# Where VectorE takes the first image's attention reciprocals: behind 62 and 68 tap operations, or behind 92 and 98

## The chip, the cores and the metric

The kernel runs on one core of a Trainium2 chip. The metric is the device time of one execution in microseconds (us), as the median of several runs. The engines are TensorE (PE, its weight loads PEld), VectorE (DVE), ScalarE (ACT), GpSimd (POOL) and SyncE (SP, which issues the DMAs).

## What is computed

Eight images x of 256 channels and 32 x 32 pixels pass through a multi-scale linear attention and a feed-forward part with routed experts. Cut to what matters here:

```python
qkv = conv2d(x_normed, qkv_w)                         # 1x1, 768 channels
agg = conv2d(qkv, agg_dw_w, groups=768, padding=2)    # 5x5 taps, channel by channel
agg = conv2d(agg, agg_pw_w, groups=96)                # 1x1 within groups of 8
ms = jnp.concatenate([qkv, agg], axis=1)              # raw half, aggregated half
q, k = relu(t[..., :8]), relu(t[..., 8:16]); v = t[..., 16:]
v = jnp.concatenate([v, ones], axis=-1)
kv = jnp.einsum('bhnd,bhne->bhde', k, v)
out = jnp.einsum('bhnd,bhde->bhne', q, kv)
out = out[..., :-1] / (out[..., -1:] + EPS_ATT)
x = x + batch_norm(conv2d(out, proj_w))
t = t + sum_e weight[b, e] * (gelu(norm(t) @ W1[e] + b1[e]) @ W2[e] + b2[e])
```

The last component of `out` is the denominator of the attention. In the kernel its reciprocals are those that the change moves.

## The kernel before, in words

The program is written engine by engine. Each engine has its own list of instructions, and they meet through semaphores. One list, `ORDER`, made by `schedule()`, gives the order of the pieces of work, and PE, ACT and POOL each walk through it and do their own part of each piece. Every piece that goes through PSUM uses one of two banks (`wbk`) in turn: PE fills it, ACT drains it. So what comes late on PE holds up all that stands behind it in the list.

DVE doesn't follow `ORDER`. It does the 5 x 5 taps. The six channel tiles m of an image are worked on in three pairs, in the order 1, 2, 0 (`PAIRS`): m = 2, 3, then m = 4, 5, then m = 0, 1. For each tap and each m of the pair there is one operation, `tap_ops(s)`, numbered n from 0. In the first image (s = 0) pair 1 is 52 operations (0 to 51), pair 2 is 40 (52 to 91) and pair 0 is 40 (92 to 131). Except for pair 1 of the first image, some taps (`base`) are made by ACT and POOL into `dwo`, and the centre operation of each m (L1104) takes them in. The other taps (L1112) add to `dacc` in PSUM; the last two of each m write `dwo`. A few small tasks stand between the taps at fixed numbers: `OF_LAST` gives those of the image before, `OF_THIS` those of this image. `("rden", h, c)` is `rden_task` (L1013 to L1016): it waits until the attention products `att` of half h (0 raw, 1 aggregated) and of four token blocks c have been drained by ACT, and takes the reciprocal of `den` for them.

```python
def rden_task(s, h, c):
    dve.wait_ge(bank_drained, drained(("att", s, h, (c + 1) * (CH // P) - 1)))
    tl = slice(c * (CH // P), (c + 1) * (CH // P))
    nc.vector.reciprocal(den[:, tl], den[:, tl]).then_inc(rden_made[h], 1)
```

What waits for it: POOL's `scale_att` (L910) multiplies `kt` by the reciprocals, and PE's `back` (L618) transposes the product, which ACT drains (L807). In the first image `ORDER` goes on, for PE and ACT, in this sequence:

1. `att` of the raw half (PE L611, ACT L803 and L804), `scale`, `back` of the raw half
2. `agg` of m = 2, 3 (PE L584), which reads DVE's pair 1
3. `qkv` of m = 2, 3 of the next image (PE L533, ACT L781), the norm of the image after that (POOL L867, L869, PE L635, POOL L875 to L883, PE L644, POOL L889), with base taps of the next image (ACT L700 and L705, POOL L924 and L930) in between
4. `agg` of m = 4, 5, which reads DVE's pair 2, and `qkv` of m = 4, 5 of the next image
5. `kv` of the aggregated half (PE L599, ACT L799), with the next image's base taps, and its mask (POOL L901, L902)
6. `agg` of m = 0, 1 (PE L579, ACT L788), which reads DVE's pair 0, then `att` of the aggregated half, `scale`, `qkv` of m = 0, 1, `back`, `proj` and so on

The feed-forward work of an image (PE L533 and L546, ACT L825, L730 and L731, POOL L960) is filled in between such pieces from the second image on.

On DVE, operations 16 and 21 of the next image have the reciprocals of the aggregated half (`OF_LAST`) ahead of them. POOL's part of `ORDER` holds the scales, the base adds, the norm's sums and products and the mask, in the same sequence. DMAs play no part around the change: the loads of x have their own waits and are issued by SP.

Of the kernel before, what the change touches and what calls it, by code (L numbers as in the profile page):

```python
# [64 lines left out]
def base_taps(s, m):  # L65

    return (0 if m in (2, 3) else len(BASE_TAPS)) if s == 0 else 3
# [8 lines left out]
def tap_ops(s):  # L76

    return [(pair, tap, m) for pair in PAIRS for tap in tap_order(s, pair) for m in (2 * pair, 2 * pair + 1)]
# [200 lines left out]
def taps_before(s, pair):  # L279

    done = sum(len(tap_ops(i)) for i in range(s))
    return done + sum(2 * len(tap_order(s, p)) for p in PAIRS[:PAIRS.index(pair)])
# [33 lines left out]
def build(nc, x, w_qkv, w_dw, w_pw, w_proj, bn, bn_rows, w_router, w1, b1, w2, b2, parts, out):  # L316
    with ExitStack() as ctx:
# [133 lines left out]
        def drained(it):  # L451

            return FILL[it] + 1

        def clip(tap):

            dy, dx = tap // TAPS - TAPS // 2, tap % TAPS - TAPS // 2
            oy, iy, ny = max(0, -dy), max(0, dy), HH - abs(dy)
            ox, ix, nx = max(0, -dx), max(0, dx), WW - abs(dx)
            return (slice(oy, oy + ny), slice(ox, ox + nx)), (slice(iy, iy + ny), slice(ix, ix + nx))  # L460
# [504 lines left out]
        def _(dve):  # L965
# [47 lines left out]
# [5 lines that stand above are left out]
            def max_task(s):  # L1018

                dve.wait_ge(bank_drained, drained(("logits", s)))  # L1020
                dve.sem_inc(dve_gate, 1)
                nc.vector.max(mx[:], lg[:]).then_inc(route, 1)
                dve.wait_ge(route, s * ROUTE + 1)
                dve.sem_inc(dve_gate, 1)
                nc.vector.max_index(ix[:], mx[:], lg[:]).then_inc(route, 1)
                nc.vector.tensor_scalar(rt[:, 0:1], mx[:, 0:1], -1.0, None, ALU.mult).then_inc(max_made, 1)

            def route_task(j):

                dve.wait_ge(exp_made, j * 2 + 2)  # L1030
                nc.vector.reciprocal(rt[:, 4:5], rt[:, 1:2]).then_inc(route, 1)
                dve.wait_ge(route, j * ROUTE + 3)

                nc.vector.tensor_scalar(rt[:, 6:8], rt[:, 2:4], rt[:, 4:5], None, ALU.mult, ALU.add,
                                        accum_out=rt[:, 8:9]).then_inc(route, 1)
                nc.vector.tensor_copy(rt[:, 12:14], ix[:, 0:2]).then_inc(route, 1)
                dve.wait_ge(route, j * ROUTE + 5)
                nc.vector.reciprocal(rt[:, 9:10], rt[:, 8:9]).then_inc(route, 1)
                dve.wait_ge(route, j * ROUTE + 6)
                nc.vector.tensor_scalar(rt[:, 10:12], rt[:, 6:8], rt[:, 9:10], None, ALU.mult).then_inc(route, 1)  # L1040
                dve.wait_ge(route, j * ROUTE + 7)
                for i in range(2):
                    ins = nc.vector.tensor_scalar(wsel[:, i, :], iota11[:], rt[:, 12 + i:13 + i], rt[:, 10 + i:11 + i],
                                                  ALU.is_equal, ALU.mult)
                ins.then_inc(route, 1)
                dve.wait_ge(route, j * ROUTE + 8)
                nc.vector.tensor_tensor(wsel[:, 0, :], wsel[:, 0, :], wsel[:, 1, :], ALU.add).then_inc(route, 1)
                dve.wait_ge(route, j * ROUTE + 9)

            def ew_task(j, par):  # L1050
                nc.vector.tensor_tensor(ewt[:], pws[:], wsel[:, 0, :].unsqueeze(1).to_broadcast([P, FT + E, NP_]),
                                        ALU.mult).then_inc(ew_chain, 1)
                dve.wait_ge(ew_chain, j * 2 + 1)
                nc.vector.reduce_sum(ewr[:], ewt[:], axis=AX_X).then_inc(ew_chain, 1)
                dve.wait_ge(ew_chain, j * 2 + 2)

                nc.vector.scalar_tensor_tensor(out=ews[par][:], in0=ewr[:], scalar=1e-6, in1=ewr[:],
                                               op0=ALU.is_gt, op1=ALU.mult).then_inc(route, 1)
                dve.wait_ge(route, j * ROUTE + 10)
                nc.vector.tensor_tensor(obt[:], b2s[:], ews[par][:, FT:FT + E].unsqueeze(1).to_broadcast([P, CT, E]),  # L1060
                                        ALU.mult).then_inc(route, 1)
                dve.wait_ge(route, j * ROUTE + 11)
                nc.vector.reduce_sum(obs[par][:], obt[:], axis=AX_X).then_inc(route, 1)
                dve.wait_ge(route, j * ROUTE + 12)
                nc.vector.tensor_scalar(ewg[par][:], ews[par][:], G_SCALE, None, ALU.mult).then_inc(route, 1)  # L1065

            def small_task(what, s):
                if what[0] == "rden":
                    rden_task(s, what[1], what[2])
                elif what[0] == "max":  # L1070
                    max_task(s)
                else:
                    route_task(s)
                    ew_task(s, s % 2)


            OF_LAST = {16: ("rden", 1, 0), 21: ("rden", 1, 1), 76: ("max",), 84: ("route",)}
            OF_THIS = {62: ("rden", 0, 0), 68: ("rden", 0, 1)}

            for s in range(B + 1):  # L1080
                if s == B:
                    for n in sorted(OF_LAST):
                        small_task(OF_LAST[n], s - 1)
                    continue
                for n, (pair, tap, m) in enumerate(tap_ops(s)):
                    if n in OF_LAST and s > 0:
                        small_task(OF_LAST[n], s - 1)
                    if n in OF_THIS:
                        small_task(OF_THIS[n], s)
                    no = taps_before(s, PAIRS[0]) + n  # L1090
                    a3 = dacc[:, m % 2, :].rearrange("p (y x) -> p y x", x=WW)
                    o3 = dwo[:, m, :].rearrange("p (y x) -> p y x", x=WW)
                    i3 = qkvs[:, m, :].rearrange("p (y x) -> p y x", x=WW)
                    if no > 1:

                        dve.wait_ge(taps, no - 1)
                    if tap is None:
                        ins = nc.vector.tensor_copy(o3[:, :, WW - 1:WW], a3[:, :, WW - 1:WW])
                    elif tap == CENTER:
                        w = dww[:, m, tap:tap + 1]  # L1100
                        if base_taps(s, m):

                            dve.wait_ge(tap_added, BASE_NO[s, m, base_taps(s, m) - 1])
                            ins = nc.vector.scalar_tensor_tensor(out=dacc[:, m % 2, :], in0=qkvs[:, m, :], scalar=w,  # L1104
                                                                 in1=dwo[:, m, :], op0=ALU.mult, op1=ALU.add)
                        else:
                            dve.wait_ge(bank_drained, drained(("qkv", s, m, NCH - 1)))
                            ins = nc.vector.tensor_scalar(dacc[:, m % 2, :], qkvs[:, m, :], w, None, ALU.mult)
                    else:
                        (oy, ox), (jy, jx) = clip(tap)  # L1110
                        dst = o3 if tap == LAST_TAP else a3
                        ins = nc.vector.scalar_tensor_tensor(  # L1112
                            out=dst[:, oy, ox], in0=i3[:, jy, jx], scalar=dww[:, m, tap:tap + 1],
                            in1=a3[:, oy, ox], op0=ALU.mult, op1=ALU.add)
                    ins.then_inc(taps, 1)
# [60 lines left out]
```

## Time and profile before

| | |
|---|---|
| median of 3 runs | 1648.99 us (1647.67 to 1650.25) |
| the profiled execution, its own time | 1651.42 us |
| its span | 1649.7 us |
| mean granted TensorE clock | 0.934 |
| busy: PE, DVE, ACT, POOL | 1360.8, 1278.6, 1063.1, 972.8 us |
| share of the span | 82%, 78%, 64%, 59% |

The profile is of one execution. The span is what the trace covers; the execution's own time is 1.7 us longer. A busy PE is not PE at its peak, since matmuls overlap. A timeline row gives the start, the length, the engine, the line, the operation with its tiles and how many were merged; in brackets, how long the engine was idle before it and what released it.

### The profile page before, as it was taken

The numbers are of one execution on the slowest core, as the hardware profiler recorded it, in microseconds if no ns is written. First come the engines' busy times: TensorE is split into PE (matmuls) and PEld (weight loads), VectorE is DVE, ScalarE is ACT, GpSimd is POOL, SyncE is SP. The second block draws the span as 40 slices with busy tenths as digits, with TensorE's granted clock in tenths as the row PEclk, the third lists the DMA queues.
The fourth block names the chain that finished last, engine by engine and source line by source line (L and its number), as shares of the span: only waits on it lengthen the run. The fifth ranks groups of instructions, "written<-read, shape, count | busy, mean of one in ns | idle before, by whom it ended". The sixth has DMA issues, their size and how long they took to land.

```text
span 1649.7 us, 18712 instructions
## 1 busy us (share of the span) xinstructions
PE 1360.8 (82%) x6844; PEld 786.7 (48%) x6844; DVE 1278.6 (78%) x1305; ACT 1063.1 (64%) x1855; POOL 972.8 (59%) x746
## 2 busy tenths in 40 slices
PE   4516647799888988799888988899888997999598
PEld 2315525455455545455455545555464445545343
DVE  4895999997969966996969966996969987970000
ACT  3434534677567775767567776777567866675476
POOL 3683626576487566576477566676476647444544
PEclk8756879899999999999999999899999999999899
DMA  5100000000001000010001100010001000100000
GB/s 180 77 2 25 26 0 1 1 27 13 1 1 39 31 9 1 0 64 14 1 1 39 39 1 1 1 39 13 1 1 39 13 1 1 39 13 1 0 14 26
DMA packets 14251, 32.75 MB, mean 20 GB/s; under 512 B 2384, under 2 KB 5328, under 8 KB 13904
## 3 DMA queue, kind: packets, MB, share of 16 engines
q1 hardware_dynamic: 14160, 31.56, 5.5%
q8 instruction: 54, 0.88, 0.2%
q14 instruction: 37, 0.30, 0.1%
HBM read 23.17 MB, written 8.39 MB: 19 GB/s over the span
## 4 chain that ended last, share of the span: by engine, by line
PE 46%; DVE 19%; ACT 19%; POOL 9%; issue 6%; DMA 1%; SPq 0%; POOLq 0%; ACTq 0%; DVEq 0%
PE wbk L533 19%; DVE dacc L1112 15%; PE acc L546 11%; PE wbk L625 6%; ACT gh L730 4%; ACT hb L731 4%; POOL dwo L930 3%; PE wbk L635 3%; ACT tapb L705 2%; POOL nrm L889 1%; PE wbk L584 1%; ACT hb L825 1%; PE wbk L611 1%; ACT dwo L700 1%; PE wbk L599 1%
## 5 line engine op out<-in xcount | busy, mean ns | idle before, releaser
L1112 DVE SCALAR_TENSOR_TENSOR dacc<-qkvs,dww,dacc 128x930 f32<-128x930 f32 (+4 forms) x954 | 1053.2, 1186 | 0.0
L960 POOL TENSOR_TENSOR gl<-hb,gh 128x512 f16<-128x512 f32 x256 | 304.4, 1191 | 419.1 <-ACT hb L731 418.2
L825 ACT ACTIVATE hb<-wbk,b1s 128x512 f32<-128x512 f32 x256 | 175.2, 684 | 156.3 <-PE wbk L533 156.2
L930 POOL TENSOR_TENSOR dwo<-dwo,tapb 128x992 f32<-128x992 f32 (+1 forms) x104 | 240.4, 2311 | 12.9 <-ACT tapb L705 9.7
L546 PE MATMUL acc<-gh,w2h 128*128 128x512 f16 x512 | 197.6, 386 | 33.5 <-ACT sum_b L764 30.6
L546 PE MATMUL acc<-gh,w2l 128*128 128x512 f16 x512 | 197.9, 387 | 0.0
L546 PE MATMUL acc<-gl,w2h 128*128 128x512 f16 x512 | 197.9, 386 | 0.0
L730 ACT ACTIVATE gh<-hb,ewg 128x512 f16<-128x512 f32 x256 | 182.3, 712 | 9.5 <-DVE ewg L1065 9.5
L533 PE MATMUL wbk<-th,w1h 128*128 128x512 f16 x512 | 154.2, 383 | 33.7 <-ACT qr L807 16.7
L731 ACT ACTIVATE hb<-hb,ewg 128x512 f32<-128x512 f32 x256 | 181.8, 710 | 0.0
L1016 DVE RECIPROCAL den<-den 128x128 f32<-128x128 f32 x32 | 30.4, 949 | 189.1 <-ACT den L804 189.1
L533 PE MATMUL wbk<-tl,w1h 128*128 128x512 f16 x512 | 153.5, 382 | 0.0
L533 PE MATMUL wbk<-th,w1l 128*128 128x512 f16 x512 | 153.4, 381 | 0.0
L705 ACT ACTIVATE tapb<-qkvs,dww 128x1024 f32<-128x1024 f32 x104 | 118.2, 1143 | 23.0 <-POOL dwo L930 20.0
L781 ACT ACTIVATE qkvs<-wbk 128x512 f32<-128x512 f32 x96 | 56.5, 594 | 73.6 <-PE wbk L533 73.6
L546 PEld LDWEIGHTS acc<-gh,w2h 128*128 128x128 f16 x512 | 50.6, 99 | 99.6 <-issue 37.6
L910 POOL TENSOR_TENSOR kt<-kt,den 128x1024 f32<-128x1024 f32 x32 | 62.7, 1968 | 59.6 <-DVE den L1016 59.6
L611 PE MATMUL wbk<-kvm,qr 128*128 128x144 f32 x512 | 81.9, 300 | 18.1 <-ACT den L804 12.9
L948 POOL TENSOR_TENSOR yr<-yr,sum_b 128x512 f32<-128x512 f32 x32 | 40.8, 1276 | 88.4 <-ACT sum_b L810 87.5
L1104 DVE SCALAR_TENSOR_TENSOR dacc<-qkvs,dww,dwo 128x1024 f32<-128x1024 f32 x46 | 87.0, 1934 | 0.0
L611 PEld LDWEIGHTS wbk<-kvm,qr 128*128 128x128 f32 x512 | 70.8, 193 | 31.6 <-ACT den L804 21.0
L533 PEld LDWEIGHTS wbk<-th,w1h 128*128 128x128 f16 x512 | 45.9, 98 | 83.8 <-ACT qr L807 20.0
(146 smaller groups left out, 2232.1 us busy)
## 6 DMA issues: line engine op xcount, KB each, us to landing
xa<-x SPq DMA_DIRECT2D x8, 1024.0 KB, 5.0
yr<-x SPq DMA_DIRECT2D x8, 1024.0 KB, 5.0
out<-yr SPq DMA_DIRECT2D x16, 512.0 KB, 2.8
dwo<-w SPq DMA_DIRECT2D x1, 2048.0 KB, 11.0
yr<-w SPq DMA_DIRECT2D x2, 1024.0 KB, 16.3
dwo<-w_qkv SPq DMA_DIRECT2D x1, 768.0 KB, 4.7
wp<-w_proj SPq DMA_DIRECT2D x1, 512.0 KB, 12.4
pw<-w_pw SPq DMA_DIRECT2D x16, 24.0 KB
```

The lines of the kernel that those rows point to most:

```text
L533: last = nc.tensor.matmul(dst, w[:, k, m * P:(m + 1) * P], d[:, k, c * CH:(c + 1) * CH], start=(i == 0), stop=(i == len(parts) - 1))
L546: last = nc.tensor.matmul(acc[:, m, :], w[:, t, m * P:(m + 1) * P], d[:, f % GB, :], start=(t == 0 and i == 0), stop=(t == FT - 1 and i == 2),
L611: last = nc.tensor.matmul(b[:, g * RD:(g + 1) * RD], qr[:, g, t * P:(t + 1) * P], kvm[:, g, :], start=True, stop=True)
L625: last = nc.tensor.matmul(b[:], wp[:, k, m * P:(m + 1) * P], (ac, qr)[k // CT][:, k % CT, c * CH:(c + 1) * CH], start=(k == 0), stop=(k == ...
L705: ins = nc.scalar.activation(tapb[:, i % 2, :], qkvs[:, m, :], ACT.Copy, scale=w)
L730: nc.scalar.activation(gh[:, f % GB, :], hb[:, f % GB, :], ACT.Copy, scale=w).then_inc(g_high, 1)
L731: nc.scalar.activation(hb[:, f % GB, :], hb[:, f % GB, :], ACT.Copy, scale=w).then_inc(g_scaled, 1)
L825: last = nc.scalar.activation(hb[:, f % GB, :], b[:], ACT.Gelu, bias=b1s[:, f % FT:f % FT + 1], scale=1.0 / (X_SCALE * W_SCALE))
L930: ins = nc.gpsimd.tensor_tensor(d3[:, oy, ox], d3[:, oy, ox], t3[:, iy, ix], ALU.add)
L960: nc.gpsimd.tensor_tensor(gl[:, f % GB, :], hb[:, f % GB, :], gh[:, f % GB, :], ALU.subtract).then_inc(g_low, 1)
L1104: ins = nc.vector.scalar_tensor_tensor(out=dacc[:, m % 2, :], in0=qkvs[:, m, :], scalar=w, in1=dwo[:, m, :], op0=ALU.mult, op1=ALU.add)
L1112: ins = nc.vector.scalar_tensor_tensor(out=dst[:, oy, ox], in0=i3[:, jy, jx], scalar=dww[:, m, tap:tap + 1], in1=a3[:, oy, ox], op0=ALU.mu ...
```

## The change

For the first image alone, the two reciprocals of the raw half stand ahead of tap operations 92 and 98 in place of 62 and 68. All other images keep 62 and 68.

```diff
             OF_LAST = {16: ("rden", 1, 0), 21: ("rden", 1, 1), 76: ("max",), 84: ("route",)}
             OF_THIS = {62: ("rden", 0, 0), 68: ("rden", 0, 1)}
+            OF_FIRST = {92: ("rden", 0, 0), 98: ("rden", 0, 1)}
...
-                    if n in OF_THIS:
-                        small_task(OF_THIS[n], s)
+                    if n in (OF_FIRST if s == 0 else OF_THIS):
+                        small_task((OF_FIRST if s == 0 else OF_THIS)[n], s)
```

The added line moves the numbers of all lines behind it by one: the centre operation is L1104 before and L1105 after, the taps are L1112 and L1113.

The first place is DVE's list at the start of pair 2 of the first image: the centre operations, then the taps. `den` holds the denominators. Before:

```order
L1104 SCALAR_TENSOR_TENSOR dacc<-qkvs,dww,dwo 128x1024 x2
L1112 SCALAR_TENSOR_TENSOR dacc<-qkvs,dww,dacc 128x30x30 x2
L1112 SCALAR_TENSOR_TENSOR dacc<-qkvs,dww,dacc 128x30x31 x4
L1112 SCALAR_TENSOR_TENSOR dacc<-qkvs,dww,dacc 128x30x30 x2
L1016 RECIPROCAL den<-den 128x128
L1112 SCALAR_TENSOR_TENSOR dacc<-qkvs,dww,dacc 128x31x30 x2
L1112 SCALAR_TENSOR_TENSOR dacc<-qkvs,dww,dacc 128x31x31 x4
L1016 RECIPROCAL den<-den 128x128
L1112 SCALAR_TENSOR_TENSOR dacc<-qkvs,dww,dacc 128x31x30 x2
```

After:

```order
L1105 SCALAR_TENSOR_TENSOR dacc<-qkvs,dww,dwo 128x1024 x2
L1113 SCALAR_TENSOR_TENSOR dacc<-qkvs,dww,dacc 128x30x30 x2
L1113 SCALAR_TENSOR_TENSOR dacc<-qkvs,dww,dacc 128x30x31 x4
L1113 SCALAR_TENSOR_TENSOR dacc<-qkvs,dww,dacc 128x30x30 x2
L1113 SCALAR_TENSOR_TENSOR dacc<-qkvs,dww,dacc 128x31x30 x2
L1113 SCALAR_TENSOR_TENSOR dacc<-qkvs,dww,dacc 128x31x31 x4
L1113 SCALAR_TENSOR_TENSOR dacc<-qkvs,dww,dacc 128x31x30 x2
```

Both reciprocals have left this stretch, and the taps stand one behind the other.

The second place is DVE's list at the end of pair 2 and the start of pair 0 of the same image. Before:

```order
L1112 SCALAR_TENSOR_TENSOR dwo<-qkvs,dww,dacc 128x32x31 x2
L1098 COPY dwo<-dacc 128x32 x2
L1104 SCALAR_TENSOR_TENSOR dacc<-qkvs,dww,dwo 128x1024 x2
L1112 SCALAR_TENSOR_TENSOR dacc<-qkvs,dww,dacc 128x30x30 x2
L1112 SCALAR_TENSOR_TENSOR dacc<-qkvs,dww,dacc 128x30x31 x4
L1112 SCALAR_TENSOR_TENSOR dacc<-qkvs,dww,dacc 128x30x30 x2
```

After:

```order
L1113 SCALAR_TENSOR_TENSOR dwo<-qkvs,dww,dacc 128x32x31 x2
L1099 COPY dwo<-dacc 128x32 x2
L1016 RECIPROCAL den<-den 128x128
L1105 SCALAR_TENSOR_TENSOR dacc<-qkvs,dww,dwo 128x1024 x2
L1113 SCALAR_TENSOR_TENSOR dacc<-qkvs,dww,dacc 128x30x30 x2
L1113 SCALAR_TENSOR_TENSOR dacc<-qkvs,dww,dacc 128x30x31 x2
L1016 RECIPROCAL den<-den 128x128
L1113 SCALAR_TENSOR_TENSOR dacc<-qkvs,dww,dacc 128x30x31 x2
```

The first reciprocal is now ahead of the centre operations of pair 0, the second behind these and four more taps. The lists of PE, ACT and POOL hold the same instructions in the same order before and after.

## Rows read from the trace of the kernel before

**Rows 1.** Windows, middle: stretch, us, busy us of PE, PEld, DVE, ACT, POOL, PEclk, DMA

```profile
330.00:1500.00 1170.00, 1053.98 (x5417) 605.07 (x5417) 993.87 (x1014) 821.37 (x1464) 727.85 (x560) 0.98 0.04 16
```

**Rows 2.** DVE's waits, whole run: us in total, times, the longest in us

```profile
DVE den L1016 <- ACT den L804: 189.1, 15, 19.9
```

**Rows 3.** Timeline of DVE: start us, us, engine, line, operation, tiles, count, [idle before <-releaser]

```profile
146.05 0.95 DVE L1016 RECIPROCAL den<-den 128x128 f32<-128x128 f32 x1 [19.88 <-ACT den L804]
146.92 6.70 DVE L1112 SCALAR_TENSOR_TENSOR dacc<-qkvs,dww,dacc 128x930 f32<-128x930 f32 x6
153.53 0.95 DVE L1016 RECIPROCAL den<-den 128x128 f32<-128x128 f32 x1
154.39 21.95 DVE L1112 SCALAR_TENSOR_TENSOR dacc<-qkvs,dww,dacc 128x930 f32<-128x930 f32 x20
...
178.81 4.53 DVE L1104 SCALAR_TENSOR_TENSOR dacc<-qkvs,dww,dwo 128x1024 f32<-128x1024 f32 x2
...
223.06 2.49 DVE L1104 SCALAR_TENSOR_TENSOR dacc<-qkvs,dww,dwo 128x1024 f32<-128x1024 f32 x2
...
240.77 0.95 DVE L1016 RECIPROCAL den<-den 128x128 f32<-128x128 f32 x1
...
318.77 0.15 DVE L1031 RECIPROCAL rt<-rt 128x1 f32<-128x1 f32 x1
```

**Rows 4.** Timeline of PE, 140 to 260

```profile
156.66 1.94 PE L618 MATMUL wbk<-ident,kt 128*128 128x128 f32 x8 [6.40 <-POOL kt L910]
...
198.36 3.73 PE L599 MATMUL wbk<-vt,kt 128*128 128x129 f32 x32
223.30 5.57 PE L579 MATMUL wbk<-dwo,pw 128*128 128x512 f32 x8 [21.20 <-DVE dwo L1098]
229.64 5.18 PE L611 MATMUL wbk<-kvm,qr 128*128 128x144 f32 x32 [0.78 <-ACT qr L788]
...
250.25 1.94 PE L618 MATMUL wbk<-ident,kt 128*128 128x128 f32 x8 [4.53 <-POOL kt L910]
```

**Rows 5.** Detail of L1104 from 176 to 184: durations in ns, shortest, median, longest

```profile
L1104 DVE SCALAR_TENSOR_TENSOR dacc<-qkvs,dww,dwo x2: 1293/2312/3331, 178.8 to 180.0; 128x1024 f32<-128x1024 f32 x2
```

**Rows 6.** Timeline of POOL, 140 to 260

```profile
154.55 1.97 POOL L910 TENSOR_TENSOR kt<-kt,den 128x1024 f32<-128x1024 f32 x1 [5.50 <-DVE den L1016]
...
176.69 5.56 POOL L930 TENSOR_TENSOR dwo<-dwo,tapb 128x992 f32<-128x992 f32 x2
182.21 1.18 POOL L875 TENSOR_TENSOR sv<-st 128x8 f32<-128x8 f32 x1
183.47 0.20 POOL L877 TENSOR_TENSOR sv<-st,sv 128x8 f32<-128x8 f32 x1
...
186.04 4.74 POOL L930 TENSOR_TENSOR dwo<-dwo,tapb 128x992 f32<-128x992 f32 x2
...
208.53 0.27 POOL L902 TENSOR_SCALAR kvm<-hm,kvr 128x16 f32<-128x16 f32 x1
```

**Rows 7.** Timeline of ACT, 140 to 260

```profile
208.90 1.15 ACT L705 ACTIVATE tapb<-qkvs,dww 128x1024 f32<-128x1024 f32 x1 [0.25 <-POOL dwo L924]
...
232.50 0.19 ACT L804 ACTIVATE den<-wbk 128x32 f32<-128x32 f32 x1
```

**Rows 8.** Windows with PE's granted clock (PEclk, as a share of 2.4 GHz)

```profile
164.00:172.00 8.00, 5.24 (x25) 2.16 (x22) 8.00 (x9) 5.11 (x8) 0.02 (x1) 1.00 0.01 2
192.00:204.00 12.00, 10.09 (x68) 7.15 (x66) 12.00 (x11) 7.38 (x13) 4.79 (x4) 1.00 0.29 89
...
224.00:228.00 4.00, 4.00 (x7) 1.51 (x6) 4.00 (x5) 1.21 (x3) 0.00 (x0) 0.62 0.00 0
```

**Rows 9.** Chain that ended last, 300 to 345: start us, us, what

```profile
310.11 8.75 DVE dacc L1112 x8
...
326.08 2.33 POOL rb L867
```

## The prediction

> **What bounds the kernel now.** I read the views from coarse to fine. The windows first: in the long middle of the run, 1170 us, TensorE (PE) is busy for 1054 and VectorE (DVE) for 994 [rows 1]. The middle is a steady pattern in which PE has little room, so a change in the first image can pay only by starting that pattern earlier or later, not by making it shorter. Then DVE's waits: nearly all its idle time in the middle is spent ahead of a reciprocal of `den`, 189.1 us in 15 waits, and the longest of these, 19.9 us, is the one this change is about [rows 2]. DVE's timeline shows it: the reciprocal at 146.05 stands behind 19.88 us of idle time [rows 3]. It is reached in order, before tap operation 62, when the attention products it needs don't exist yet. 30 tap operations of the same pair, which need nothing from it, are queued behind it.
>
> The question is what hangs on the reciprocals. The first scale of `kt` on GpSimd (POOL), the `back` transposes on PE, and behind them in PE's fixed order everything up to `att` of the aggregated half wait for them. Before the change that chain has slack: after `kv` of the aggregated half starts at 198.36, PE has no more to do until DVE ends pair 0 at 223.06, and the row at 223.30 shows PE idle for 21.20 us for that [rows 4]. So there are two paths with opposite shifts. DVE's own taps come earlier, the chain through POOL, PE and ACT comes later, and they meet at DVE's operation 16 of the next image, the reciprocal at 240.77, which needs `att` of tokens 0 to 3.
>
> **The change, term by term.** Times are of the profiled execution (span 1649.7, its own time 1651.42); the three timed runs have the median 1648.99, which is 2.43 below it. I work out a shift and take it off the median.
>
> *DVE, pair 2 (gain).* Operation 62 ran at 146.92, behind 19.88 idle and 0.87 of a reciprocal (146.05 to the next start) [rows 3]. Without both it starts at 146.92 - 20.75 = 126.2. Operations 62 to 91 take (153.53 - 146.92) + (178.81 - 154.39) = 31.0 us, so pair 2 ends at 157.2 in place of 178.8.
>
> *The first reciprocal* is due at 157.2; its input was there at 146.0, so no wait.
>
> *Operations 92 to 97* are two centre operations (L1104) and four taps. Four taps are 4 x 1.10 = 4.4 (21.95 for 20) [rows 3]. The pair of centres took 4.53 at 178.81 and 2.49 at 223.06: a price from 2.5 to 4.5. The detail shows 1.29 and 3.33 for the two at 178.81 [rows 5], and POOL's timeline has tensor operations on it at that time, two adds from 176.69 on, and none is shown at 223.06 [rows 6]. The first scale (1.97) now becomes free just as the centres start, so I take 4.45, the row it is nearest to. The Trainium skill, "SBUF — State Buffer", section "Who interferes with whom", says that a VectorE instruction with two SBUF inputs and a GpSimd one that reads SBUF exclude each other, the second waiting for the whole of the first: by that the pair is two free centres and one scale, 2.49 + 1.97 = 4.5, and by the undisturbed row alone it would be 2.5, the chain below 2 us earlier and the forecast 2 us lower. By that rule, the trace agrees (1.29 and 3.33).
>
> *The second reciprocal* is then at 157.2 + 0.87 + 4.45 + 4.4 = 166.9, in place of 153.53: the chain is **13.3 us later** from here. Pair 0 ends at 223.06 - 19.9 = 203.1: DVE's path is **19.9 us earlier**. The two reciprocals cost DVE 2 x 0.87 in either place.
>
> *The chain.* The second scale goes from 154.55 to 167.9, the second pair of `back` from 156.66 to 170.0, with `agg` of m = 2, 3 behind it [rows 6, 4]. Every piece keeps its length but one place. POOL's two adds at 176.69 took 5.56, where the same two at 186.04 took 4.74, and the 8-element operation at 182.21 took 1.18, where its like at 183.47 took 0.20 [rows 6]: both ran beside the centres of 178.81, which are no longer there. That is 0.8 + 1.0 = 1.8 back, if none of it is lost to something else. The chain is from there +11.5 (bounds: 13.3 with no relief, 9.5 with undisturbed centres as well). `kv` of the aggregated half moves from 198.36 to 209.9. The mask on POOL ended at 208.53 + 0.27 = 208.8 and now ends at 220.3 [rows 6].
>
> *A new place in line.* `agg` of m = 0, 1 no longer waits for DVE (203.1), nor much for PE (free at 213.6). Its first bank is drained by ACT, and ACT stands in order behind its last base-tap copy (208.90, 1.15 long), which waits for POOL's memset behind the mask [rows 7]. So the first drain starts at 210.0 + 11.5 = 221.5. With two banks, two of the four products are done by then, and two remain after the first drain (0.6). The four took 5.57 in all [rows 4], and the mean granted clock was 0.62 of 2.4 GHz from 224 to 228, that is 1.2 GHz at first [rows 8]. PE will have been idle again, so I take the slower level, two of four at 1.7 each (the first 3.7 us of the row at half rate, 1.9 at full: 0.93 each at full, 1.86 at half; both ends 2 to 3.7). 222.1 + 3.4 = 225.5, the last drain 0.6, `att` at about 226.3 in place of 229.64, so 3.3 earlier. The four `den` pieces were there at 232.69 (232.50 + 0.19) [rows 7], and are now at 229.4.
>
> *The meeting.* DVE arrives at operation 16 at 240.77 - 19.9 = 220.9. Its two centres of this image (203.1) may collide with POOL's next pass over `xa`, which follows the adds of 186.04 and is moved to 202.2: 2.49 as at 223.06, or up to 6.3 with both held. Either is covered, since arrival is then at most 224.7, below 229.4. So a **new wait of 5 to 9 us** stands there, and DVE goes on at 229.4 in place of 240.77: **11.3 us earlier**. If the cover were gone, each microsecond of the collision would count.
>
> *What follows.* The second scale is 6.4 + 3 later, at 238.8, and the second pair of `back` starts at about 239.2 in place of 250.25, where PE sat idle for POOL 4.53 us [rows 4]. That is 11.0 earlier for the chain, 11.3 for DVE. Later waits in the second image keep their distances, for both sides move together. The chain of work that ended last runs on DVE's taps to 318.8, through the routing behind it at 318.77 and then POOL's sum at 326.08 into the steady pattern [rows 3, 9], and all of this is moved alike. The loads of x were issued long before. Sum: -19.9 + 8.9 = **-11.0 us**, so 1651.4 becomes 1640.4, and the median 1649.0 becomes **1638.0**.
>
> **The rivals.**
> *A, the forecast*: 11.0 less, 0.70. Its ends: no relief on POOL and dearer `agg` give 8.9; cheap centres give 13. One stretch of PE at the other clock level is worth up to 3 more. Its own range is 1634 to 1643.
>
> *B, nothing is handed on:* the whole 19.9 arrives, 1629.1. This needs `att` of the aggregated half by 220.9, before the mask (220.3) and the drains behind it allow. 0.04.
>
> *C, the gain is mostly lost where the steady pattern begins:* if not DVE but PE's position decides from 230 on, the 3.3 us of `att` are all that arrive, 1645.7, and with 2 us more in the chain 1647.6: no change. For it speaks PE's share in the middle [rows 1]; against it PE's idle 4.53 for POOL at 250.25 and a chain that runs on DVE until 318 [rows 4, 9]. 0.17.
>
> *D, slower:* TensorE stays at 1.2 GHz through the chain. The engine is busy for 5.24 and 10.09 us at full clock in 164 to 172 and 192 to 204 [rows 8], and it got there each time after a stretch of work that followed an idle one. The idle time ahead of the second `back` grows from 6.4 to about 8. If it doubles those 15.3 us, `den` comes at 229.4 + 15.3 = 244.7 in place of 232.69, DVE goes on 3.9 us later than before: 1652.9. It turns slower from 11.4 us more in the chain on. Against it: the same bursts stand at the same distances as before. The Trainium skill, "TensorE: Matmul & The Clock Gate", section "What's actually happening", calls the throttled state the default, which activity releases; that is the rule against this change, and here it gives D only if the release fails to come. 0.09.
>
> That the change doesn't do what it says has no room: on DVE's list the two reciprocals do stand around the centres of pair 0, and PE's list is the same.
>
> **The numbers.** 0.2% is 3.3 us, about what a measurement of this kernel can tell from no change: faster is below 1645.7. A and B lie there, and C half a step on either side of it: faster 0.76, same 0.15, slower 0.09. The range takes in A and most of C, 1633.5 to 1647, and leaves out B, D and C's last part.
>
> **What would show it.** No idle time on DVE near 126, a reciprocal near 157.2 and one near 166.9; pair 0 done near 203; one new wait on `den` of 5 to 9 us that ends near 229.4; PE's wait for DVE at `agg` of m = 0 gone; everything from 330 on moved by 11. Wrong is the prediction if that new wait ends after 233 or is missing, if `back` at 239 isn't earlier by about 11, or if the distance shrinks between 250 and 400.

## The result and the profile after

| | before | changed |
|---|---|---|
| median | 1649.23 us (5 runs, 1647.67 to 1650.25) | 1639.09 us (5 runs, 1637.13 to 1643.02) |
| ratio | | 0.9943, 95% interval 0.9928 to 0.9959 |
| the profiled execution, its time and span | 1651.42, 1649.7 us | 1641.19, 1639.5 us |
| mean granted TensorE clock | 0.934 | 0.935 |
| busy: PE, DVE, ACT, POOL | 1360.8, 1278.6, 1063.1, 972.8 | 1362.3, 1279.8, 1063.9, 973.1 |

The kernel is 10.1 us faster, against the 11.0 that were forecast. No engine does less work; the time was idle time. The timeline of DVE in the changed kernel, which answers to [rows 3]:

```profile
112.06 4.51 DVE L1105 SCALAR_TENSOR_TENSOR dacc<-qkvs,dww,dwo 128x1024 f32<-128x1024 f32 x2
...
156.28 0.94 DVE L1016 RECIPROCAL den<-den 128x128 f32<-128x128 f32 x1
157.14 4.11 DVE L1105 SCALAR_TENSOR_TENSOR dacc<-qkvs,dww,dwo 128x1024 f32<-128x1024 f32 x2
...
165.47 0.94 DVE L1016 RECIPROCAL den<-den 128x128 f32<-128x128 f32 x1
...
201.74 5.16 DVE L1105 SCALAR_TENSOR_TENSOR dacc<-qkvs,dww,dwo 128x1024 f32<-128x1024 f32 x2
...
227.57 0.95 DVE L1016 RECIPROCAL den<-den 128x128 f32<-128x128 f32 x1 [5.35 <-ACT den L804]
...
305.64 0.16 DVE L1031 RECIPROCAL rt<-rt 128x1 f32<-128x1 f32 x1
```

The idle row of 19.88 us at the first reciprocal is gone. Pair 2 runs in one piece from 112.06, and the first reciprocal comes at 156.28 without a wait. The second comes at 165.47, 11.9 us later than the one at 153.53 before. The new wait on `den` is there, at 227.57, and is 5.35 us long. DVE goes on 13.2 us earlier than at 240.77, and the routing starts 13.1 us earlier (305.64 against 318.77). The waits of DVE on `den` in the whole run went from 189.1 us [rows 2] to:

```profile
DVE den L1016 <- ACT den L804: 176.7, 15, 16.0
```

POOL in the changed kernel, to be laid beside [rows 6]:

```profile
166.49 1.97 POOL L910 TENSOR_TENSOR kt<-kt,den 128x1024 f32<-128x1024 f32 x1 [6.34 <-DVE den L1016]
...
187.91 4.74 POOL L930 TENSOR_TENSOR dwo<-dwo,tapb 128x992 f32<-128x992 f32 x2
192.60 0.20 POOL L875 TENSOR_TENSOR sv<-st 128x8 f32<-128x8 f32 x1
...
195.45 4.75 POOL L930 TENSOR_TENSOR dwo<-dwo,tapb 128x992 f32<-128x992 f32 x2
...
217.88 0.28 POOL L902 TENSOR_SCALAR kvm<-hm,kvr 128x16 f32<-128x16 f32 x1
```

The two adds at 187.91 now take 4.74 in place of 5.56, and the 8-element operation behind them 0.20 in place of 1.18. The mask ends at 217.88 + 0.28 = 218.2, 9.4 us later than before.

PE in the changed kernel, to be laid beside [rows 4]:

```profile
168.60 1.94 PE L618 MATMUL wbk<-ident,kt 128*128 128x128 f32 x8 [6.36 <-POOL kt L910]
170.37 4.90 PE L584 MATMUL wbk<-pw,dwo 128*128 128x128 f32 x32
...
207.68 3.73 PE L599 MATMUL wbk<-vt,kt 128*128 128x129 f32 x32
211.25 2.08 PE L579 MATMUL wbk<-dwo,pw 128*128 128x512 f32 x4
219.93 3.78 PE L579 MATMUL wbk<-dwo,pw 128*128 128x512 f32 x4 [6.60 <-ACT qr L788]
224.50 5.17 PE L611 MATMUL wbk<-kvm,qr 128*128 128x144 f32 x32 [0.78 <-ACT qr L788]
...
237.28 1.15 PE L618 MATMUL wbk<-ident,kt 128*128 128x128 f32 x8 [0.84 <-ACT qr L807]
```

PE's 21.20 us of waiting for DVE at `agg` of m = 0 is gone: two of the four products follow at once on `kv` (211.25). The other two wait 6.60 us for ACT. ACT's timeline shows what it stands behind, the last base-tap copy and then, later, the fourth piece of `den` (to be laid beside [rows 7]):

```profile
218.25 1.15 ACT L705 ACTIVATE tapb<-qkvs,dww 128x1024 f32<-128x1024 f32 x1 [0.25 <-POOL dwo L924]
...
227.35 0.19 ACT L804 ACTIVATE den<-wbk 128x32 f32<-128x32 f32 x1
```

`att` starts at 224.50, 5.1 us earlier than at 229.64, and its fourth `den` is there at 227.35 + 0.19 = 227.54. The second pair of `back` starts at 237.28, 13.0 us earlier than at 250.25.

So the first 310 us gave 13.1 us. At the end of the span only 10.2 are left. The other 3 went in two steps, and beside the larger one the granted clock is lower. The same stretch in both kernels, windows view, PEclk is the third number from the end. Before:

```profile
1370.00:1430.00 60.00, 48.18 (x278) 31.75 (x276) 47.62 (x60) 41.20 (x78) 39.60 (x30) 0.94 0.03 9
```

Changed:

```profile
1370.00:1430.00 60.00, 49.80 (x261) 30.64 (x260) 53.14 (x65) 38.78 (x75) 32.55 (x24) 0.89 0.08 27
```

The starts of the `max` operation (one for each image) tell how far ahead the changed kernel is along the run:

| | 1st `max` | 5th | 6th | 7th | 8th | end of the span |
|---|---|---|---|---|---|---|
| before | 309.50 | 1045.36 | 1229.88 | 1405.60 | 1546.14 | 1649.7 |
| changed | 296.37 | 1032.24 | 1217.78 | 1393.52 | 1535.80 | 1639.5 |
| ahead by | 13.1 | 13.1 | 12.1 | 12.1 | 10.3 | 10.2 |

The lead is constant up to the fifth. It loses 1.0 between the fifth and the sixth, and 1.7 between the seventh and the eighth, 142.28 us in place of 140.54. The two windows above don't hold the same work, since the changed kernel is 12 us ahead. Laid by the work, from 12 us ahead of the seventh `max` to 24 behind it, the mean clock is 0.91 before and 0.81 in the changed kernel. What the step of 1.0 comes from is open.

### The profile page after: what moved, and what is told of

It reads as the page before. It is cut to its first block, busy times and chain, and to the rows that moved or that the text cites. A ratio compares the mean times of both kernels' runs of the same rounds, so it can differ in the third digit from the quotient of the medians.

```text
span 1639.5 us, 18712 instructions
## 1 busy us (share of the span) xinstructions
PE 1362.3 (83%) x6844; PEld 786.6 (48%) x6844; DVE 1279.8 (78%) x1305; ACT 1063.9 (65%) x1855; POOL 973.1 (59%) x746
## 4 chain that ended last, share of the span: by engine, by line
PE 46%; DVE 20%; ACT 17%; POOL 8%; issue 8%; DMA 1%; POOLq 0%; SPq 0%; ACTq 0%; DVEq 0%
PE wbk L533 20%; DVE dacc L1113 17%; PE acc L546 10%; PE wbk L625 6%; ACT gh L730 4%; ACT hb L731 3%; ACT tapb L705 2%; PE wbk L584 2%; POOL dwo L930 2%; PE wbk L635 2%; POOL gl L960 2%; PE wbk L579 1%; ACT dwo L700 1%; PE wbk L611 1%; ACT sum_b L810 1%
## 5 line engine op out<-in xcount | busy, mean ns | idle before, releaser
L1113 DVE SCALAR_TENSOR_TENSOR dacc<-qkvs,dww,dacc 128x930 f32<-128x930 f32 (+4 forms) x954 | 1053.2, 1189 | 0.0
L930 POOL TENSOR_TENSOR dwo<-dwo,tapb 128x992 f32<-128x992 f32 (+1 forms) x104 | 240.2, 2309 | 13.4 <-ACT tapb L705 10.2
L1105 DVE SCALAR_TENSOR_TENSOR dacc<-qkvs,dww,dwo 128x1024 f32<-128x1024 f32 x46 | 88.0, 1957 | 0.0
```

Source lines behind the costliest of these rows:

```text
L930: ins = nc.gpsimd.tensor_tensor(d3[:, oy, ox], d3[:, oy, ox], t3[:, iy, ix], ALU.add)
L1113: ins = nc.vector.scalar_tensor_tensor(out=dst[:, oy, ox], in0=i3[:, jy, jx], scalar=dww[:, m, tap:tap + 1], in1=a3[:, oy, ox], op0=ALU.mu ...
```

## The experiments

The experiments change only numbers in the tables of VectorE's small tasks. `S` below is the start of pair 2's centres on DVE (112.06 in the changed kernel); positions counted from S leave out what the setup took in an execution.

### 82 and 86

```diff
-            OF_FIRST = {92: ("rden", 0, 0), 98: ("rden", 0, 1)}
+            OF_FIRST = {82: ("rden", 0, 0), 86: ("rden", 0, 1)}
```

Expected: 

> First image: the two reciprocals ahead of tap operations 82 and 86. Two-path theory: the stall of 19.88 us was DVE arriving too early for data that is there at 146 to 147, and operation 82 is reached at about 125.1 + 20 x 1.1 = 147.1, so there is no wait, and the second reciprocal comes at about 152.4, no later than the 153.53 of the kernel before. The chain through POOL and PE is then not delayed, its mask ends at about 208, den is there some 9.4 us behind it (218.1 to 227.54 in the changed kernel), at about 217.3, and DVE, which reaches operation 16 of the second image at about 219, doesn't wait. Nearly the whole stall is gained: den at operation 16 starts at 219 to 220 in place of 240.77, the time is 1628 to 1631. Rival (the gain is capped by PE's position, not by the meeting with DVE): 1635 to 1640, as the changed kernel. Rival (it matters only that the reciprocals leave 62): same as the changed kernel, 1639.

Measured: 1631.40 us (4 runs), ratio to the kernel before 0.9875 (0.9851 to 0.9899). DVE's timeline:

```profile
147.47 0.94 DVE L1016 RECIPROCAL den<-den 128x128 f32<-128x128 f32 x1
...
152.62 0.94 DVE L1016 RECIPROCAL den<-den 128x128 f32<-128x128 f32 x1
...
158.08 2.49 DVE L1105 SCALAR_TENSOR_TENSOR dacc<-qkvs,dww,dwo 128x1024 f32<-128x1024 f32 x2
...
200.29 5.30 DVE L1105 SCALAR_TENSOR_TENSOR dacc<-qkvs,dww,dwo 128x1024 f32<-128x1024 f32 x2
...
220.83 0.94 DVE L1016 RECIPROCAL den<-den 128x128 f32<-128x128 f32 x1
```

There is no wait at either place: the reciprocals come at 147.47 and 152.62, and that of operation 16 at 220.83 without idle time. ACT had written the last `den` that this one needs at 217.85, so the chain had 3.0 us to spare. The reciprocals don't have to be moved to the end of the pair to fill the stall. They have to be moved by 20 operations. Every one more delays the chain; how far that is free, the run with 88 and 92 tells. The centres of pair 0 (158.08) have no scale beside them and take 2.49. This kernel beats both others. It was run again beside the last experiment: 1630.47 (5 runs), 0.9882 (0.9863 to 0.9902). The first of the two times lies 0.4 above the upper end of what was expected, the second inside. Operation 16 comes 0.8 later than expected: the centres of the second image (200.29) met POOL and took 5.30.

### 62 and 98

```diff
-            OF_FIRST = {92: ("rden", 0, 0), 98: ("rden", 0, 1)}
+            OF_FIRST = {62: ("rden", 0, 0), 98: ("rden", 0, 1)}
```

Expected: 

> First image: the first reciprocal stays at 62, only the second moves to 98. The stall of about 19.9 us stays, and the chain behind the second reciprocal starts at about 185 to 187 in place of 153.53, some 31 us later. Two-path theory: the mask ends at about 238, den of the aggregated half is there at about 247.5, DVE waits for it some 7 to 9 us at operation 16 of the second image, and the kernel is slower than before by 5 to 8 us: 1654 to 1657. Rival (DVE's own path alone decides, the chain has slack enough): 1647 to 1650, no difference.

Measured: 1658.96 us (5 runs), ratio 1.0055 (1.0037 to 1.0072): slower than before. DVE's timeline:

```profile
144.77 0.95 DVE L1016 RECIPROCAL den<-den 128x128 f32<-128x128 f32 x1 [19.83 <-ACT den L804]
...
183.45 0.94 DVE L1016 RECIPROCAL den<-den 128x128 f32<-128x128 f32 x1
...
246.16 0.95 DVE L1016 RECIPROCAL den<-den 128x128 f32<-128x128 f32 x1 [5.42 <-ACT den L804]
```

The stall of 19.83 stays and the second reciprocal comes at 183.45. `den` comes at 246.1, and DVE waits 5.42 us for it (7 to 9 expected), 5.4 us later than at 240.77. Counted from S it is 6.7 later (136.3 against 129.6 us), since S is 109.88 here and was 111.15 before. The delay of the chain alone costs, and nothing hides it once the meeting is later than before. The profiled execution took 1657.28 us, 5.9 more than that of before, which is what the later meeting costs. The median is 9.3 above that of before and 2 above the expectation (1654 to 1657); the sign and the place are as the theory had them, the rest of the size, 2.6, is open. That DVE's own path alone decides is refuted.

### 82 and 98

```diff
-            OF_FIRST = {92: ("rden", 0, 0), 98: ("rden", 0, 1)}
+            OF_FIRST = {82: ("rden", 0, 0), 98: ("rden", 0, 1)}
```

Expected: 

> First image: first reciprocal at 82, second at 98 as in the change. Two-path theory: the second reciprocal starts the chain, so the time is near that of the changed kernel. The port collision moves: POOL's first scale now runs near 148 and no longer beside the centre operations of pair 0, so these take 2.5 us in place of 4.1 us, the second reciprocal is 1.6 us earlier than 165.47, at about 163.9, and the wait on den ends about 1.6 us before 227.57: 1637 to 1638. Rival (the first reciprocal's scale and back start the chain): as with 82 and 86, 1628 to 1631. Rival (no port collision): centres at 4.1 as before, 1639.

Measured: 1641.07 us (4 runs), ratio 0.9933 (0.9909 to 0.9958), the same as the changed kernel. So it is the second reciprocal that starts the chain, not the first. The time is 3.1 above the expected range (1637 to 1638). The first `max` (294.06) is 15.4 ahead of that of before, the end of the span only 8.9: of the 6.5 lost behind it, 4.2 lie between the seventh and the eighth `max`.

The collision moved as expected, and the second reciprocal came 51.7 us behind S in place of 53.4. Detail of L1105 at pair 0 in the changed kernel, in ns (shortest, median, longest); in this run both centres took 1289 to 1294 ns:

```profile
L1105 DVE SCALAR_TENSOR_TENSOR dacc<-qkvs,dww,dwo x2: 1209/2099/2989, 157.1 to 158.3; 128x1024 f32<-128x1024 f32 x2
```

But the 1.6 us weren't handed on: counted from S, operation 16 has its `den` at 115.5 us in both. PE's timeline shows where they stayed. This run first, then a repeat of the changed kernel with nearly the same S (109.77 and 109.85):

```profile
164.62 1.94 PE L618 MATMUL wbk<-ident,kt 128*128 128x128 f32 x8 [15.47 <-POOL kt L910]
166.39 5.65 PE L584 MATMUL wbk<-pw,dwo 128*128 128x128 f32 x32
...
192.14 3.75 PE L644 MATMUL wbk<-spread,sv 128*128 128x128 f32 x16 [3.52 <-POOL sv L883]
```

```profile
166.37 1.94 PE L618 MATMUL wbk<-ident,kt 128*128 128x128 f32 x8 [6.36 <-POOL kt L910]
168.15 4.91 PE L584 MATMUL wbk<-pw,dwo 128*128 128x128 f32 x32
...
193.16 2.82 PE L644 MATMUL wbk<-spread,sv 128*128 128x128 f32 x16 [3.97 <-POOL sv L883]
```

The second `back` is 1.75 us earlier, but `agg` behind it takes 5.65 in place of 4.91 and the broadcast of the norm (L644) 3.75 in place of 2.82. PE's clock did not rise earlier because its work did: in both, the mean granted clock from 164 to 172 is 0.61. Taken in steps of 2 us it is 0.50 in both from 168 to 170 and 0.94 here and 0.93 in the repeat from 170 to 172, so it rose at the same time although `back` and `agg` had begun 1.75 us earlier here. From 184 to 198 it is 0.64 here and 0.76 in the repeat. The earlier start was spent at 1.2 GHz. This compares one execution with one.

### 104 and 110

```diff
-            OF_FIRST = {92: ("rden", 0, 0), 98: ("rden", 0, 1)}
+            OF_FIRST = {104: ("rden", 0, 0), 110: ("rden", 0, 1)}
```

Expected: 

> First image: the reciprocals ahead of 104 and 110, 12 tap operations (13.2 us) later than in the change. DVE's own path is the same as in the changed kernel. Two-path theory: the centres of pair 0 run without POOL's scale beside them (2.5 us), so the second reciprocal comes at about 165.5 + 13.2 - 1.6 = 177, den at operation 16 at about 227.6 + 11.6 = 239, and the gain is all but gone: 1647 to 1649. Rival (all that counts is that DVE doesn't stall at 62): 1639 as the changed kernel. Rival (chain has slack to 240 on PE but other waits grow with it): over 1650.

Measured: 1653.44 us (10 runs), ratio 1.0020 (1.0009 to 1.0031). DVE's timeline:

```profile
176.74 0.94 DVE L1016 RECIPROCAL den<-den 128x128 f32<-128x128 f32 x1
...
204.46 1.29 DVE L1105 SCALAR_TENSOR_TENSOR dacc<-qkvs,dww,dwo 128x1024 f32<-128x1024 f32 x1 [4.55 <-POOL dwo L930]
213.01 3.29 DVE L1105 SCALAR_TENSOR_TENSOR dacc<-qkvs,dww,dwo 128x1024 f32<-128x1024 f32 x1 [7.26 <-POOL dwo L930]
...
240.06 0.95 DVE L1016 RECIPROCAL den<-den 128x128 f32<-128x128 f32 x1 [8.44 <-ACT den L804]
```

The second reciprocal comes at 176.74 (177 expected), and the wait on `den` of 8.44 us ends at 240.06 (239 expected), within 1 us of 240.77 before. DVE doesn't stall at 62 here, and yet the gain is gone. A wait appeared that had not been forecast: the two centres of the next image stood idle 4.55 and 7.26 us for POOL's base adds, which stand behind the delayed chain. They cost nothing more, since DVE would have waited for `den` anyway. The time is 4 to 6 us above what was expected, and 3.8 above that of before. By the number alone it is the second rival's (over 1650, other waits grow with the chain), and waits did grow, but these two are covered. The start of the first `max` is 308.80, 0.7 ahead of before, while the profiled execution took 2.1 more, so these 3 us arise later. The steps from one `max` to the next show 1.0 of it between the fourth and the fifth, 0.4 behind that and 1.4 between the seventh and the eighth. The mean granted clock from 1370 to 1600 is 0.93 here against 0.96 before; that this is their cause was not tried.

### 68 and 74

```diff
-            OF_FIRST = {92: ("rden", 0, 0), 98: ("rden", 0, 1)}
+            OF_FIRST = {68: ("rden", 0, 0), 74: ("rden", 0, 1)}
```

Expected: 

> First image: reciprocals ahead of 68 and 74, six tap operations (6.6 us) later than before. Two-path theory: DVE fills 6.6 us of the stall of 19.9 with taps, so the stall is about 13.3, the first reciprocal stays at about 146, the second at about 153.5, the chain isn't delayed, and there is no wait at operation 16: everything from there on 6.6 us earlier, time 1642 to 1644. Rival (the stall is charged to whoever comes late on PE, so the chain decides and stays where it was): 1649, no difference.

Measured: 1645.86 us (9 runs), ratio 0.9963 (0.9948 to 0.9977).

```profile
145.88 0.95 DVE L1016 RECIPROCAL den<-den 128x128 f32<-128x128 f32 x1 [13.21 <-ACT den L804]
...
236.02 0.94 DVE L1016 RECIPROCAL den<-den 128x128 f32<-128x128 f32 x1
```

The stall is 13.21 (13.3 expected), and operation 16 is reached 4.8 us earlier, without a wait. The expectation had 6.6. The centres of pair 0 (at 171.95) took 6.63 in this run in place of 4.53, which accounts for 2.1 of it: they came earlier and met two of POOL's operations (171.85 and 174.17) that had not moved. Taps that fill a stall also change what they run beside. The time is 2 us above the expected range: the median gained 4.3 on this chip.

### 88 and 92

```diff
-            OF_FIRST = {92: ("rden", 0, 0), 98: ("rden", 0, 1)}
+            OF_FIRST = {88: ("rden", 0, 0), 92: ("rden", 0, 1)}
```

Expected: 

> First image: reciprocals ahead of 88 and 92. Counted from the start of pair 2's centres on DVE (112.06 in the changed kernel), DVE reaches operation 16 of the second image 110.2 us later, and den was there after 115.5 us with the second reciprocal at 53.4. Here the second reciprocal comes at about 47.1, 6.3 us earlier, so den is there after about 109.2: the two paths meet just about where DVE arrives. Two-path theory with a threshold: no wait or under 1 us, operation 16 at 110 to 111 us, time 1631 to 1634, nearly that of 82 and 86. Rival (the time falls evenly with the place of the second reciprocal between 98 and 86): operation 16 at 112 us, 1635 to 1636, with a wait of about 2 us.

Measured: 1630.64 us (4 runs), ratio 0.9877 (0.9862 to 0.9892), as with 82 and 86.

```profile
157.00 0.94 DVE L1016 RECIPROCAL den<-den 128x128 f32<-128x128 f32 x1
...
219.54 0.95 DVE L1016 RECIPROCAL den<-den 128x128 f32<-128x128 f32 x1
```

S is 109.96, so the second reciprocal stands at 47.0 us and operation 16 at 109.6, with no wait. The two paths meet here: ACT's last `den` for this reciprocal is there at 219.51, and DVE's taps end at 219.48. The time (0.4 below the expected 1631 to 1634) doesn't fall evenly from 98 to 86: it is flat up to 92 and rises behind it, as two paths that meet would have it.

### 66 and 71 in all other images

```diff
-            OF_THIS = {62: ("rden", 0, 0), 68: ("rden", 0, 1)}
-            OF_FIRST = {92: ("rden", 0, 0), 98: ("rden", 0, 1)}
+            OF_THIS = {66: ("rden", 0, 0), 71: ("rden", 0, 1)}
+            OF_FIRST = {82: ("rden", 0, 0), 86: ("rden", 0, 1)}
```

Expected, first run: 

> First image at 82 and 86, and in all other images the raw half's reciprocals ahead of 66 and 71 in place of 62 and 68. In the middle of the run DVE waits about 13 us there in each of five images (12.96 at 454.42 in the run with 82 and 86), so four more taps (4.4 us) run under the wait, the second reciprocal comes 1.1 us earlier, and the max and the routing behind it come 4.4 us earlier. The chain of work runs through these. Theory that DVE's path through the routing decides there too: up to 4.4 us for each of five images, 1609 to 1622. Rival (PE is the bound in the middle and the waits on den are only its shadow): 1629 to 1633, no difference to 82 and 86 alone. Rival (in the second image, where DVE doesn't wait, the reciprocals are late by 4.4 and 3.3 us): 1 to 4 us of loss.

Measured: 1627.34 us (4 runs, 1625.10 to 1635.08), ratio 0.9859 (0.9821 to 0.9898). DVE's timeline in the third image:

```profile
453.85 0.95 DVE L1016 RECIPROCAL den<-den 128x128 f32<-128x128 f32 x1 [8.52 <-ACT den L804]
...
467.62 0.18 DVE L1022 MAX8 mx<-lg 128x8 f32<-128x16 f32 x1 [0.92 <-ACT lg L818]
```

DVE's wait shrank from 12.96 to 8.52 us, just by the four taps, and a new wait of 0.92 for the logits stands ahead of the `max`. From this `max` to the next are 183.9 us, and 184.6 with 82 and 86 alone. The time lies 5 above the theory's range (1609 to 1622) and 1.7 below that of the rival with PE as the bound (1629 to 1633). To tell 4 us from the scatter, both kernels were run again side by side. The other of the two:

> 82 and 86 in the first image once more, beside the kernel with 66 and 71 in all other images, on the same chip. Expected 1628 to 1632.

and this one:

> 82 and 86 in the first image and 66 and 71 in all others once more. If the 4 us between the two medians (1631.4 and 1627.3) were real, it is 2 to 5 us faster again than 82 and 86 alone on the same chip. Rival (PE bounds the middle, a difference of a few us is the scatter of TensorE's clock): within 2 us.

Measured: 1630.47 and 1629.26 us (5 runs each), ratios 0.9882 (0.9863 to 0.9902) and 0.9887 (0.9870 to 0.9904). They are 1.2 apart, within the 2 of the rival: no difference that can be told. The traces show more than the sums. From the first to the seventh `max` the two traces with 66 and 71 took 1092.2 and 1092.3 us, and the two with 82 and 86 alone 1096.2 both, so the middle became 4 us shorter, twice. From the seventh to the eighth they took 144.1 against 140.6 and 141.0, and most of it was lost again; why, was not tried. DVE's waits on `den` fell from 169.2 to 150.8 us in all, and its waits for the logits ahead of the `max` and for ACT at L1031 rose by 10 together. So in the middle these waits are mostly the shadow of PE: some 18 us less of them gave 4 us there and nothing that can be told at the end.

### The changed kernel twice more

No edit. Expected: 

> The changed kernel once more. Theory that the 13.2 us gained by operation 16 of the second image are fixed by the order of work, and that the 3 us lost again behind 1380 are a matter of where TensorE's stretches at the lower clock fall: the wait on den at operation 16 ends again 13 to 14 us ahead of the kernel before, while the part from 1380 on differs by up to 3 us. Rival (the loss at the end belongs to the change): the same shift, 10, at the end each time.

and 

> The changed kernel once more, the same expectation as for the first repeat; two repeats tell whether the late part varies between executions.

Measured, one execution each: 1635.99 and 1638.15 us. The wait on `den` in the first repeat:

```profile
225.34 0.95 DVE L1016 RECIPROCAL den<-den 128x128 f32<-128x128 f32 x1 [5.35 <-ACT den L804]
```

It is 5.35 us long as in the profiled run, 5.33 in the second, and ends 115.5 and 115.3 us behind S, 115.5 in the profiled run. This part is fixed by the order of work. It ends 15.4 and 16.0 us ahead of the kernel before and not 13 to 14 as expected, because S itself came 2.2 and 2.6 us earlier (109.85 and 109.44) than in the profiled run. The late part isn't fixed. The first repeat is 15.4 us ahead of the kernel before at this place (225.34 against 240.77), 15.5 at the seventh `max` (1390.08), and 15.4 at the end of its span (1634.3). It lost nothing, and its window reads:

```profile
1370.00:1430.00 60.00, 49.56 (x264) 30.09 (x265) 56.59 (x68) 40.15 (x77) 32.68 (x21) 0.94 0.08 27
```

The second was 16.0 ahead here (224.74) and 13.3 at the end (1636.4): it lost 1.1 between the fifth and the sixth `max` and 1.7 between the seventh and the eighth, as the profiled run did. So both steps of the loss come and go between executions of one program.

The clock goes with the second step. Eleven traces here, that of before among them, leave all images but the first as they were. Laid by the seventh `max` as above, five of them (before, the first repeat, both of 82 and 86, 62 and 98) have a mean clock of 0.91 and 140.5 to 141.1 us from the seventh to the eighth. The other six have 0.81 and 142.0 to 142.3 us, and 144.8 with 82 and 98. Nothing was run that sets the clock, so that it is the cause is argued from this.

## Why the prediction was right

It gave 1638.0 and a range of 1633.5 to 1647.0; 1639.09 was measured. By its own steps:

| step | forecast | measured |
|---|---|---|
| operation 62 starts | 126.2 | 125.11 |
| first reciprocal, no wait | 157.2 | 156.28 |
| centres of pair 0 | 4.45 | 4.11 |
| second reciprocal | 166.9 | 165.47 |
| chain's delay after POOL's relief (mask) | +11.5 | +9.4 |
| third and fourth product of `agg` | 3.4 | 3.78 |
| `den` of token 3 there | 229.4 | 227.54 |
| DVE arrives at operation 16 | 220.9 to 224.7 | 222.2 |
| new wait | 5 to 9 | 5.35 |
| DVE from there on | -11.3 | -13.2 |
| second pair of `back` | -11.0 | -13.0 |
| everything from 330 on | -11 | -13.1, at the end -10.2 |

*The removal of the stall* was right, and so was *that it isn't all gained*. 82 and 86, 62 and 98, and 104 and 110 show the two paths each by itself.

*The chain* was 2.1 us less late than forecast. The terms of that are in the rows. The profiled run of before took 6.39 us for pair 2's centres, the changed one 4.51, and started them 0.9 later. The rows of before are

```profile
111.15 6.39 DVE L1104 SCALAR_TENSOR_TENSOR dacc<-qkvs,dww,dwo 128x1024 f32<-128x1024 f32 x2
110.94 5.51 POOL L930 TENSOR_TENSOR dwo<-dwo,tapb 128x992 f32<-128x992 f32 x2 [1.20 <-ACT tapb L705]
```

That makes 1.0 which doesn't come from the moved reciprocals. What decides it is which engine starts first: in the five traces in which POOL's add began ahead of these centres, as here, they took 6.3 to 6.6, and in the eight in which DVE began first (112.06 against 112.75 in the changed kernel) they took 4.5. All three traces of the changed kernel have 4.5. Before the change the stall behind them hid the price; now they stand on the path. `agg` behind the second `back` took 4.90 in place of 5.62, 0.7, since the clock rose earlier relative to it: over `agg` the mean granted clock was 0.78 in place of 0.67. The centres of pair 0 took 0.3 less. Together 2.0. POOL's relief was 0.8 and 1.0, as forecast.

*The collision of the centres with POOL* was priced rightly where it stood on the path (4.11, one held). The pair in the second image took 5.16 in place of the undisturbed 2.49, inside the bounds, and DVE's arrival at 222.2 shows it was covered. Its detail, in ns:

```profile
L1105 DVE SCALAR_TENSOR_TENSOR dacc<-qkvs,dww,dwo x2: 1877/2624/3370, 201.7 to 203.5; 128x1024 f32<-128x1024 f32 x2
```

The Trainium skill, "SBUF — State Buffer", section "Who interferes with whom", has a VectorE instruction with two SBUF inputs and a GpSimd one that reads SBUF exclude each other, the second waiting for the whole of the first. The trace agrees: beside one scale the centres took 1209 and 2989 ns and the scale 2.85 us in place of 1.97, and they took 1289 to 1294 ns each where the scale was moved away.

*What follows*, "all of this is moved alike", is the step that was off. It held up to the fifth `max`. Behind it 3 us were lost in the profiled execution and in the second repeat, and nothing in the first repeat, whose window from 1370 to 1430 has the clock of before. Rival A named this size ("one stretch of PE at the other clock level is worth up to 3 more") but as a bound, and the forecast had no term for it. So that the median came out within 1.1 us of the forecast is in part luck: two deviations cancel, a gain in the first 310 us that is 2 larger, half of it by the shorter centres of pair 2, and a loss at the end that the forecast didn't have.

*The rivals.* B (all 19.9 arrives) is refuted by the wait of 5.35, and the run with 82 and 86 shows that it needs a chain without delay: 18.2 to 19.8 us on the medians. C (PE's position decides from 230 on) is refuted by the second `back`, which is 13.0 us ahead while `att` is only 5.1 ahead. D (slower, with TensorE at 1.2 GHz through the chain) didn't occur. The run with 62 and 98 shows its other half: a chain that is later without the gain on DVE does cost.

## What to carry to other kernels

When an in-order engine stalls on a small task with independent work behind it, move the task just behind as many operations as fill the stall, and further only within the slack of what waits for it. Here the first reciprocal moved by 20 operations (the second by 18) gave 18 to 20 us, by 26 (24) 20, both by 30 10, and both by 42 lost 4. Before moving it, find where its consumers' chain and the engine's own path meet again; the gain is the engine's lead up to that meeting, and the chain's delay beyond its slack is paid in full. A wait in a stretch that another engine bounds is hardly such a place: there the same trick took 18 us from the waits in all, made the stretch 4 us shorter and left no difference in the time that can be told.

## What the hardware showed that was not expected

TensorE's clock can swallow an earlier arrival. With 82 and 98 the chain started 1.75 us earlier than in the repeat of the changed kernel, and nothing of it was left at the wait on `den`: the granted clock was 0.50 in both up to 170, so the earlier work ran at 1.2 GHz. The same program's executions differ by some us, and the clock goes with part of it: the seven of the changed kernel lie between 1635.99 and 1643.02, and the profiled one with 0.89 from 1370 to 1430 lost 1.7 us between the seventh and the eighth `max` where a repeat with 0.94 lost 0.5.

Two engines that hold each other up cost different amounts by which of them starts first. The same two centres beside the same two adds of POOL took 6.39 us where the add had begun 0.2 us ahead of them, and 4.51 where it began 0.7 us behind.
